# Attention with text and image keys: both projections from fp32r pairs to scaled fp16 pairs

## The reference

```python
residual = hidden_states
sm_scale = 1.0 / jnp.sqrt(D)
q = _split_heads(hidden_states @ Wq.T, H)
k = _split_heads(text @ Wk.T, H)
v = _split_heads(text @ Wv.T, H)
out = _merge_heads(_attend(q, k, v, sm_scale))   # softmax(q k^T * sm_scale) v
out = out @ Wo.T + bo
return out + residual
```

## Time and profile before

| | us |
|---|---|
| median of 3 runs | 434.07 (433.29 to 434.44) |
| the profiled execution's own time | 434.35 |
| its span in the trace | 432.6 |
| PE busy | 424.6 (98%) |
| PE weight loads busy | 310.7 (72%) |
| POOL busy | 301.0 (70%) |
| ACT busy | 253.9 (59%) |
| DVE busy | 231.6 (54%) |

### The profile page before, as it was taken

One profiled execution on the slowest core, in us unless ns is written; L12 is line 12 of the kernel. 1 busy time (PEld: TensorE's weight loads), 2 busy tenths in 40 slices (PEclk: granted clock), 3 DMA queues, 4 the chain that ended last, 5 costly groups with the idle time before them and its releaser, 6 DMA issues.

```text
span 432.6 us, 8258 instructions
## 1 busy us (share of the span) xinstructions
PE 424.6 (98%) x2538; PEld 310.7 (72%) x2538; DVE 231.6 (54%) x437; ACT 253.9 (59%) x509; POOL 301.0 (70%) x256
## 2 busy tenths in 40 slices
PE   8999989999999999999999999999999999999996
PEld 6877765577776777777777677777777767777775
DVE  0354785655555555555555555555555555555623
ACT  1638887757465755748464755757564755755510
POOL 8337798999658765969659674969659684865460
PEclk9999999999999999999999999999999999999999
DMA  8998536444454346543455335643355333444203
GB/s 280 353 327 266 210 110 220 150 149 145 137 197 157 134 156 204 192 146 125 145 184 184 124 131 205 205 168 124 124 192 192 128 122 137 156 159 161 76 24 121
DMA packets 39614, 72.68 MB, mean 168 GB/s; under 512 B 5024, under 2 KB 6176, under 8 KB 39584
## 3 DMA queue, kind: packets, MB, share of 16 engines
q1 hardware_dynamic: 28784, 52.62, 34.6%
q10 hardware_dynamic: 10800, 19.67, 14.1%
HBM read 28.81 MB, written 10.49 MB: 91 GB/s over the span
## 4 chain that ended last, share of the span: by engine, by line
PE 89%; DMA 3%; SPq 2%; ACT 2%; POOL 1%; DVE 1%; issue 1%; POOLq 0%; ACTq 0%
PE ps_q L672 30%; PE ps_o L672 27%; PE ps_s L734 10%; PE ps_pv L741 7%; PE ps_m L720 5%; PE ps_den L746 4%; PE ps_o L655 2%; DMA x_f<-in_x 2%; PE ps_m L787 1%; DMA q_packed<-mxT 1%; PE ps_m L725 1%; PE ps_q L787 1%; SPq L264 1%; DVE x_f L576 1%; PE ps_o L787 1%
## 5 line engine op out<-in xcount | busy, mean ns | idle before, releaser
L336 POOL TENSOR_TENSOR p_lo<-p_f,p_hi 77x512 f16<-77x512 f32 x160 | 183.9, 1168 | 99.7 <-ACT p_hi L430 97.3
L426 ACT ACTIVATE p_f<-ps_s 77x512 f32<-77x512 f32 x160 | 94.7, 592 | 45.7 <-PE ps_s L734 45.7
L546 DVE TENSOR_REDUCE mx<-ps_m 128x4 f32<-128x308 f32 x160 | 69.3, 475 | 54.8 <-PE ps_m L720 54.6
L430 ACT ACTIVATE p_hi<-ps_s 77x512 f16<-77x512 f32 x160 | 93.5, 584 | 2.8 <-PE ps_den L746 2.7
L539 DVE TENSOR_TENSOR q_lo<-ps_q,q_hi 128x512 fp32r<-128x512 f32 x40 | 27.7, 692 | 102.6 <-ACT q_hi L412 102.6
L672 PE MATMUL ps_q<-x_hi,wq_hi 128*128 128x512 f32 x200 | 79.5, 397 | 0.7 <-POOL x_lo L327 0.3
L672 PE MATMUL ps_q<-x_lo,wq_hi 128*128 128x512 f32 x200 | 78.2, 391 | 0.0
L672 PE MATMUL ps_q<-x_hi,wq_lo 128*128 128x512 f32 x200 | 78.2, 391 | 0.0
L672 PE MATMUL ps_o<-attn_hi,wo_hi 128*128 128x512 f32 x170 | 69.7, 410 | 0.6 <-POOL attn_lo L342 0.6
L672 PE MATMUL ps_o<-attn_hi,wo_lo 128*128 128x512 f32 x170 | 66.9, 393 | 0.0
L672 PE MATMUL ps_o<-attn_lo,wo_hi 128*128 128x512 f32 x170 | 66.8, 393 | 0.0
(11 more groups left out here) (105 smaller groups left out, 517.1 us busy)
## 6 DMA issues: line engine op xcount, KB each, us to landing
q_packed<-q_hi SPq DMA_DIRECT2D x80, 256.0 KB, 2.5
x_f<-in_x SPq DMA_DIRECT2D x40, 256.0 KB, 3.4
q_packed<-q_lo SPq DMA_DIRECT2D x40, 256.0 KB, 3.2
x_res<-in_x ACTq DMA_DIRECT2D x35, 256.0 KB, 2.7
out<-out_sb ACTq DMA_DIRECT2D x35, 256.0 KB, 2.6
wk_sb<-in_wk SPq DMA_DIRECT2D x8, 320.0 KB, 5.8
wv_sb<-in_wv SPq DMA_DIRECT2D x5, 512.0 KB, 5.9
wq_sb<-in_wq SPq DMA_DIRECT2D x5, 320.0 KB, 4.8
```

The lines of the kernel that those rows point to most:

```text
L336: nc.gpsimd.tensor_tensor(p_lo[:, i, :], p_f[:, i, :], p_hi[:, i, :], ALU.subtract).then_inc(plo_done, 1)
L426: nc.scalar.activation(p_f[:, i, :], ps_s[i % 2][0:L, :], ACT.Exp, scale=SCALE).then_inc(pf_done, 1)
L430: nc.scalar.activation(p_hi[:, i, :], ps_s[i % 2][0:L, :], ACT.Exp, scale=SCALE).then_inc(phi_done, 1)
L546: nc.vector.tensor_reduce(mx[:, g % RS, :, tt], ps_m[tt % 2][:, 0:HG * L].rearrange("p (h k) -> p h k", k=L), AX_X, ALU.max).then_inc(max_ ...
```

## The change

From tile 2 on the query projection, and from tile 1 on the output projection, takes its operands as fp16 high and low parts instead of fp32r ones, still three matmuls per chunk. So that fp16's range holds, x, Wq, Wo and the attention result are scaled first: DVE takes absolute maxima per partition into tops (find_tops), PE sums them over the partitions with a matmul against a constant 2^-15 (sum_tops), DVE reads the sum (read_sums) and makes reciprocals (set_scales); ACT multiplies x in place by the reciprocal (x_scale) and each weight group too (w_half_high), and the results are scaled back where they leave PSUM (q_high, q_low, finish_out). The fp32 weights, overwritten by then, are loaded again (load_w_again). The fp16 pairs lie where the fp32r high parts lay.

The residual is finished in place: ACT adds the bias to x_res (add_bias), finish_out writes its result over it, the store reads from there, and the next residual's load waits for that store. x of the next tile but one is loaded in one go in the steps g = 3, and x of tile 7 is loaded once more for the residual of tile 7. The hardware loop of SP, POOL, ACT and DVE starts one tile later. The core of the diff:

```diff
+    def x_in_half(t):
+        return not isinstance(t, int) or t >= 2
+    def o_in_half(t):
+        return not isinstance(t, int) or t >= 1
+    def from_step(first, t, g):
+        return tuple(k for k in range(G) if isinstance(t, int) and nth(t, g) == first + k)
+    def wq_again_at(t, g):
+        return from_step(4, t, g)
+    def wo_again_at(t, g):
+        return from_step(7, t, g)
+    def x_tops_at(t, g):
+        if g == G - 1:
+            return t + 2, (0, 1)
+        return (t + 1, (2, 3, 4)) if g == 0 else (t + 1, ())
+    def has_sums(t, g):
+        if isinstance(t, int) and t < 3:
+            return G <= nth(t, g) <= 2 * G + 2
+        return g == 1 and has_next(t)
+    def x_scaled_at(t, g):
+        return t + 1 if g == 1 and has_next(t) and x_in_half(t + 1) else None
+    def wq_half_high_at(t, g):
+        return from_step(6, t, g)
+    def wo_half_high_at(t, g):
+        return {8: (0,), 9: (1,), 11: (2,), 12: (3,), 13: (4,)}.get(nth(t, g), ()) if isinstance(t, int) else ()
+    def wq_half_low_at(t, g):
+        return {6: (0,), 8: (1, 2), 9: (3,), 11: (4,)}.get(nth(t, g), ()) if isinstance(t, int) else ()
+    def wo_half_low_at(t, g):
+        return {9: (0, 1), 11: (2,), 13: (3, 4)}.get(nth(t, g), ()) if isinstance(t, int) else ()
...
-    LOOP = (2, NB - 2)
+    LOOP = (3, NB - 2)
...
             def step(t, g):
+                load_w_again(wq_sb, wq, wq_in, q_chunks, 1, wq_again_at(t, g))
+                load_w_again(wo_sb, wo, wo_in, o_chunks, 0, wo_again_at(t, g))
...
+                if g == G - 2 and (not isinstance(t, int) or 0 <= t < NB - 1):
+                    load_x(t + 2, range(G))
...
+                    if x_in_half(t):
+                        nc.gpsimd.tensor_tensor(x_16[:, c, 1, :], x_f[:, c, :], x_16[:, c, 0, :],
+                                                ALU.subtract).then_inc(xlo_pool, 1)
...
+            def x_scale(t):
+                for c in range(G):
+                    act.wait_ge(x_up_done, t - 1)
+                    nc.scalar.mul(x_f[:, c, :], x_f[:, c, :], x_up[:, :]).then_inc(x_scaled, 1)
+
+            def w_half_high(groups, w_sb, w_16, up, up_done, scaled, hi):
+                for k in groups:
+                    act.wait_ge(up_done, k + 1)
+                    nc.scalar.mul(w_sb[:, k, :], w_sb[:, k, :], up[:, k:k + 1]).then_inc(scaled, 1)
+                    act.wait_ge(scaled, k + 1)
+                    nc.scalar.copy(w_16[:, k, 0, :], w_sb[:, k, :]).then_inc(hi, 1)
+
+            def add_bias(t, k):
+                act.wait_ge(res_in[k % RS], 16 * slot_uses(t, k))
+                nc.scalar.add(x_res[:, k % RS, :], x_res[:, k % RS, :], bias[:, k:k + 1]).then_inc(res_done, 1)
...
                 if exists(slot_before(t, k)[0]):
-                    act.wait_ge(outs_done, nth(*slot_before(t, k)) + 1)
+                    act.wait_ge(out_in[k % RS], 16 * slot_uses(*slot_before(t, k)))
                 act.dma_start(x_res[:, k % RS, :], x[t, :, k, :]).then_inc(res_in[k % RS], 16)
...
+                for tile in out_tiles(t, g):
+                    if o_in_half(tile[0]):
+                        add_bias(*tile)
...
+            def largest(col, src, **flags):
+                nc.vector.tensor_reduce(tops[:, col:col + 1], src, AX_X, ALU.max, **flags).then_inc(tops_done, 1)
...
+            def read_sums(t, g):
+                dve.wait_ge(sums_done, sums_so_far(t, g))
+                nc.vector.tensor_scalar(sums[:, :], ps_sum, TINY, None, ALU.max).then_inc(sums_read, 1)
...
+                nc.tensor.matmul(ps_sum, down[:, :], tops[:, :], start=True, stop=True).then_inc(sums_done, 1)
...
-                project(ps_q, wq_hi, wq_lo, x_hi, x_lo, g, chunks, ready, q_chunks)
+                operands = halves(wq_16, x_16) if x_in_half(t) else (wq_hi, wq_lo, x_hi, x_lo)
+                project(ps_q, *operands, g, chunks, ready, q_chunks)
...
-                project(out_bank(t, k), wo_hi, wo_lo, attn_hi, attn_lo, k, chunks, ready, o_chunks)
+                operands = halves(wo_16, attn_16) if o_in_half(t) else (wo_hi, wo_lo, attn_hi, attn_lo)
+                project(out_bank(t, k), *operands, k, chunks, ready, o_chunks)
...
                 if exists(t):
                     scores(t, g, 0, batch(t))
                     scores(t, g, 1, batch(t))
+                if has_sums(t, g):
+                    sum_tops(t, g)
                 if exists(max_t):
                     max_scores(max_t, max_g, 0, batch(max_t))
                     max_scores(max_t, max_g, 1, batch(max_t))
+                if has_sums(t, g):
+                    pe.wait_ge(sums_read, sums_so_far(t, g))
                 if tiles:
                     project_out(*tiles[0], (0, 1))
```

More of the change, by code:

```diff
@@ L107, in wo_split_at, with wq_top_at, wo_top_at, is_v_top @@
         return {(0, 3): (0,), (0, 4): (1,), (1, 1): (2, 3), (1, 3): (4,)}.get((t, g), ()) if isinstance(t, int) else ()
+    def x_in_half(t):
[12 more added lines that the diff above has]
+        return (t + 1, (2, 3, 4)) if g == 0 else (t + 1, ())
+    def wq_top_at(t, g):
+        return from_step(5, t, g)
+    def wo_top_at(t, g):
+        return from_step(7, t, g)
+    def is_v_top(t, g):
+        return isinstance(t, int) and (t, g) == (0, G - 1)
+    def has_sums(t, g):
+        if isinstance(t, int) and t < 3:
+            return G <= nth(t, g) <= 2 * G + 2
+        return g == 1 and has_next(t)
+    def tops_before(t, g):
+        if not isinstance(t, int) or t >= 3:
+            return tops_before(2, G - 1) + G * (t - 2)
+        total = 0
+        for n in range(G - 1, nth(t, g)):
+            at = n // G, n % G
+            xt, chunks = x_tops_at(*at)
+            total += (len(chunks) if xt >= 2 else 0) + len(wq_top_at(*at)) + len(wo_top_at(*at)) + is_v_top(*at)
+        return total
+    def sums_so_far(t, g):
+        return nth(t, g) - G + 1 if isinstance(t, int) and t < 3 else G + 3 + t - 2
+    def x_scaled_at(t, g):
[8 more added lines that the diff above has]
+        return {9: (0, 1), 11: (2,), 13: (3, 4)}.get(nth(t, g), ()) if isinstance(t, int) else ()
     def attn_split_at(t, g):
@@ L174, in xattn_kernel @@
         ones = sb("ones", [L, D], F16)
+        down = sb("down", [P, P], F32R)
+        tops = sb("tops", [P, TOPS], F32R)
+        sums = sb("sums", [P, TOPS], F32)
+        x_sum, x_up = sb("x_sum", [P, 1], F32), sb("x_up", [P, 1], F32)
+        wq_sum, wq_up = sb("wq_sum", [P, G], F32), sb("wq_up", [P, G], F32)
+        wo_up, out_scale = sb("wo_up", [P, G], F32), sb("out_scale", [P, G], F32)
+        v_sum, v_up, v_rel = sb("v_sum", [P, 1], F32), sb("v_up", [P, 1], F32), sb("v_rel", [P, G], F32)
+        q_scale = sb("q_scale", [P, G], F32)
+        sb("places_kept", [P, D], F32)
         x_f = sb("x_f", [P, G, TB], F32)
-        x_hi = sb("x_hi", [P, G, TB], F32R)
+        with ExitStack() as first_tiles:
+            x_hi = sb("x_hi", [P, G, TB], F32R, first_tiles)
+        x_16 = sb("x_16", [P, G, 2, TB], F16)
         x_lo = sb("x_lo", [P, G, TB], F32R)
@@ L301, in step @@
                     load_w(nth(t, g) + G - 1)
-                xt = t + 2 if g == G - 1 else t + 1
-                if exists(xt) and not (isinstance(xt, int) and xt == 0):
-                    load_x(xt, {G - 1: (0, 1), 0: (2, 3), 1: (4,)}.get(g, ()))
+                if isinstance(t, int) and nth(t, g) in (-1, 0, 1):
+                    load_x(1, {G - 1: (0, 1), 0: (2, 3), 1: (4,)}[g])
+                if g == G - 2 and (not isinstance(t, int) or 0 <= t < NB - 1):
+                    load_x(t + 2, range(G))
                 for c in wo_chunks(t, g):
@@ L358, in wo_low, with w_half_low @@
                                         ALU.subtract).then_inc(wo_lo_done, 1)
+            def w_half_low(groups, w_sb, w_16, hi, lo):
+                for k in groups:
+                    pool.wait_ge(hi, k + 1)
+                    nc.gpsimd.tensor_tensor(w_16[:, k, 1, :], w_sb[:, k, :], w_16[:, k, 0, :],
+                                            ALU.subtract).then_inc(lo, 1)
             def step(t, g):
@@ new lines, in largest, with find_tops @@
+            def largest(col, src, **flags):
+                nc.vector.tensor_reduce(tops[:, col:col + 1], src, AX_X, ALU.max, **flags).then_inc(tops_done, 1)
+            def find_tops(t, g):
+                if is_v_top(t, g):
+                    dve.wait_ge(down_done, 2)
+                    dve.wait_ge(vscale_done, 3 * G)
+                    largest(V_TOP, v_scale[:, :])
+                xt, chunks = x_tops_at(t, g)
+                if exists(xt) and x_in_half(xt):
+                    for c in chunks:
+                        dve.wait_ge(x_in[c], 16 * (xt + 1))
+                        largest(c, x_f[:, c, :], apply_absolute_value=True)
+                for k in wq_top_at(t, g):
+                    dve.wait_ge(wq_in[k], 32)
+                    largest(WQ_TOP, wq_sb[:, k, :], apply_absolute_value=True)
+                for k in wo_top_at(t, g):
```

(2 more changed lines are left out.)

149 lines of the change are left out of this document (129 added, 20 removed).

## The result

The changed kernel takes 431.86 us (430.77 to 433.51, 15 runs) against 433.29 us (432.83 to 434.44, 15 runs) for the kernel before: ratio 0.9966, 95% interval 0.9955 to 0.9977. It is faster by 1.4 us, a fifth of the 7.4 us forecast. (The forecast of 426.7 us took those 7.4 us off 434.07, the median of three runs; fifteen runs give 433.29.) The profiled execution took 431.85 us, with a span of 430.0.

A forecast was written before the change was run, and what follows sets the result against it. PE's matmul slots were taken to bound the steady part, with POOL counting too in the filling part. 12.4 - 3.7 - 1.0 - 0.3 = 7.4 us of gain off 434.07 gave 426.7 us; range 420.5 to 437.

The forecast's parts named there:

- Slots: PE's fp16 projection matmuls take 0.217 us each; with a shorter weight load behind the transpose, 12.4 us of gain.
- Format changes: PE going between fp32r and fp16 around output chunks: taken as 0, with 15.6 us as the other end.
- (1): Format changes cost PE in both directions at five output-chunk borders per step: 15.6 us, time 442.3; chance 0.10.
- (2): Format changes cost PE in one direction only: in, 6 us, 432.7; out, 9.6 us, 436.3; chance 0.11.
- (5): PE's projection slot does not get shorter: 439 us; chance 0.04.
- (4): PE gains more: slots of 0.213, hidden load behind the transpose, sums hidden: 418.9, more likely 421; chance 0.10.
- The sums: Extra PE matmul of the maxima, with wait and weight load, in twelve steps: 0.31 us each, 3.7 us.
- DVE and the DMAs: DVE's absolute maxima and the repeated loads of weights and x, at a DMA share under 0.5, cost nothing.
- ScalarE: ACT's bias addition is covered; scalings plus weight casts overrun in steps 6 and 11, 0.5 us of PE wait each.
- POOL: POOL's x, attention and weight remainders barely fit their cover; 0.3 us of stall allowed for the ramp, up to 5.
- rival (3): The bound moves to POOL or ACT, late remainders or bias addition; the gain goes back, 433 to 436; chance 0.11.

The follow-up runs named there:

- sums_early: Against the new kernel, PE makes the matmul of the maxima ahead of scores 0 and 1 instead of behind them: 431.06 us.
- burst_alone: Against the kernel before, only the five x chunks of tile 2 are issued in one go in step (0, 3): 436.43 us, ratio 1.0064.
- x_wq_later: Against the new kernel, second Wq loads and, in step 4, tile 2's x chunks go behind the row-maxima DMA: 429.48 us, ratio to the kernel before 0.991.
- tops_later: Against x_wq_later, the maxima of tile 2's x chunks 0 and 1 are taken in step (1, 0): 427.87 us, ratio to the kernel before 0.9866.
- scale_spread: Against the new kernel, two of ACT's five scalings of x move into step g = 2, around exponential 2, all work kept: 431.57 us.
- tiny_bias: Against ramp_fixed, the bias is added to 8 of 512 columns of each residual only: 424.93 us beside 424.62.
- wq_later: Against the new kernel, SP issues the second load of a Wq group behind the row-maxima DMA instead of ahead of it: 431.78 us.
- ramp_fixed: The new kernel with the orders of x_wq_later, tops_later, sums_early and scale_spread together, same work: 425.16 us, again 424.62; ratios to the kernel before 0.9816, 0.9791.

## Why the prediction was wrong

**Slots: right.** 0.217 us was forecast from the fp16 strips, 0.216 measured; the steady step fell to 9.45 us, forecast about 9.4. Steps 13 to 40 gain 9.4 us, sums included.

**Format changes: right.** In the steady step the first output chunk starts 0.28 us after two max-score matmuls began (205.40, 205.68), as before, and the next entry comes 0.24 us after scores began (207.28, 207.52) instead of 0.23. The chunks and two max scores from 205.68 to 207.28 take 1.60 us, where six slots of 0.216 and two of 0.141 give 1.58. So the borders cost 0.01 to 0.02 us each, not 0.10 to 0.16. (The forecast took 0 on the strength of a single case, at the lower clock and in one direction; that it held in both had some luck in it.) And the entry to the values, fp16 on both sides now, still has its price: the last of 15 query matmuls starts at about 209.81 + 14 x 0.216 = 212.83 and the values at 213.14, 0.31 us. The change of strips costs there, not the format. Rivals (1), (2) and (5) are out, and with a slot of 0.216 and not 0.213 so is (4).

**The sums: about right.** 0.31 us a step forecast; the steps 16 and 21 with sums take 9.64, 26 and 31 take 9.79, against 9.45: 0.19 and 0.34. In sums_early all four take 9.56, 0.11 more, which is the low end of the forecast, the slot alone; what lay above it was PE's wait. The 0.1 us put down for a weight load that is no longer hidden does not show there.

**DVE and the DMAs: the step that failed.** "Weights loaded twice and x once more, 4.5 MB on 73, lie at a DMA share under 0.5: nothing." The share is a mean of stretches of 20 and 50 us, and the earlier trace rows has only those of the kernel before from 80 to 150 us; even its stretch from 60 to 80 us, where the new kernel went wrong, has a mean of 0.45. The working gave no term of its own to the move of x's loads. The part of the change that it passed over was order: five x chunks in one step, ahead of a transfer that PE waits for. Where the sum has nothing, steps 4 and 5 took 6.3 us longer, by the 3.3 us wait for the row maxima and the lower clock behind it. burst_alone shows that the x burst alone costs 3 us; x_wq_later and tops_later together recover 4.0.

**ScalarE: right mechanism, wrong size.** The overrun of the scalings with a weight group was put at 0.5 us of PE wait in each of two steps; scale_spread shows 0.95 and 1.2. The operation takes 3.17/5 = 0.63 us where the sum had 0.53, and what was queued behind q_high was not the max scores alone but q_low and, behind it, read_sums, on which the output chunks wait. The bias addition costs next to nothing, as forecast (0.3 us in tiny_bias's trace).

**POOL: right.** No wait of PE for p_lo, x_lo or attn_lo shows in the ramp, where the kernel before had three, of 0.2 to 0.3 us; the five x remainders went down to 1.16 us each, as allowed for. With the bias addition this takes out rival (3) too.

**The clock: not in the sum.** No term stands for it. Each of the gaps of 1.9 us and more (new kernel, wq_later, x_wq_later, burst_alone) brought a stretch at 1.2 GHz, and step 5 lost 2.7 us in which PE waited for less than a microsecond.

With all orders mended, ramp_fixed takes 424.6 to 425.2 us, 8.3 to 8.6 us less than before. That this lies near the forecast 7.4 does not confirm the sum: ramp_fixed also takes out most of the waits for sums and of the scalings' overrun, for which the sum had charged 4.7 us, the sums' slots included. With only the loads and the two maxima moved, as in tops_later, the gain is 5.6 us, and its profiled run still lost time to the lower clock.

## What to carry to other kernels

Write down, for each queue, what is issued between two issues of the transfer that the bottleneck waits for, before and after the change, in bytes, and whether it has landed by then; a mean DMA share says nothing about it. When a load is moved out of one reader's way, name the next one that waits for it. In a pipeline's filling steps each queue has its own slack, and an operation that is placed at the end of a step, ahead of the one that others wait for, can cost time even on an engine with room to spare.

## What the runs showed of the hardware

An 8 KB DMA issued on SP's queue behind 2.7 MB, of which the last packing and a weight group had yet to land, took 5.03 us. Behind 2.4 MB it took 3.61 us in burst_alone and, with a Wq group in place of the Wo group and another order, 3.44 in ramp_fixed and 5.07 in tops_later, so the bytes alone do not set it; with the DMA engines idle at its issue it took 1.82 us. A gap of 3.3 us on PE was followed by work at half the clock until 80.1 us, 6.5 us of it, and one of 1.9 us by a stretch of 0.73. The same kernel, ramp_fixed, kept the full clock in one profiled run, with gaps of 0.39, 0.71 and 1.15 us in steps 5 and 6, and had 0.66 over 10 us in another, with 0.69, 1.61 and 1.15; their spans differ by 3.5 us (422.4 and 425.9), more than most single edits here. Why the second step-5 gap was longer in one is open, beyond that a small DVE operation ahead of it (v_rel) took 1.12 us instead of 0.23. Between fp32r and fp16 matmuls on the whole array PE loses 0.01 to 0.02 us; between the whole array and four strips, with fp16 on both sides, 0.09.
